# A decoder layer on eight cores: the residual and layer-norm stage of a query block is split into four pieces that are placed between the projections of the next block

## What is computed

```python
cq  = layernorm(x @ W_dq) ; q = [cq @ W_uq | rope(cq @ W_qr)]      # 16 heads of 128
ckv = layernorm(x @ W_dkv); k = [ckv @ W_uk | rope(x @ W_kr)]; v = ckv @ W_uv
attn = softmax(causal(q @ k.T / sqrt(128))) @ v
x1  = layernorm(x + attn @ W_o.T)
h   = silu(x1 @ (w_gate * s_gate)) * (x1 @ (w_up * s_up))
out = layernorm(x1 + (h @ w_down) * s_down)
```

## Time and profile before

| | us |
|---|---|
| profiled execution, whole | 8303.3 |
| its span on the slowest core (core 4) | 8301.6 |
| spans of the other seven cores | 8216.7 to 8294.2 |
| two timed runs | 8458.29 and 8760.03, median 8609.16 |
| PE busy in the span | 5968.6 (72%) |
| ACT busy | 2493.1 (30%) |
| DVE busy | 1747.0 (21%) |

### The profile page before, as it was taken

One profiled execution on the slowest core, in us unless ns is written; L12 is line 12 of the kernel. 1 busy time (PEld: TensorE's weight loads), 2 busy tenths in 40 slices (PEclk: granted clock), 3 DMA queues, 4 the chain that ended last, 5 costly groups with the idle time before them and its releaser, 6 DMA issues.

```text
span 8301.6 us, 76583 instructions; the slowest of 8 cores (8216.7 to 8301.6 us)
## 1 busy us (share of the span) xinstructions
PE 5968.6 (72%) x24816; PEld 2356.7 (28%) x24816; DVE 1747.0 (21%) x2859; ACT 2493.1 (30%) x4029; POOL 833.0 (10%) x1482
## 2 busy tenths in 40 slices
PE   1555558686485288438853888399999949999992
PEld 1222223233112112111221112144444424444441
DVE  0233322100131121111111110122322242222224
ACT  1222224311271175137612775111111111111111
POOL 1000000000000000000000000021212102121220
PEclk9877778888768678768886889699999979999996
DMA  4311131323213212321133222332323243232222
GB/s 103 75 59 62 39 78 63 79 69 93 46 36 87 72 45 61 76 79 54 47 84 82 61 58 68 102 91 61 83 71 82 72 137 82 72 82 72 75 78 76
DMA packets 411044, 603.61 MB, mean 73 GB/s; under 512 B 118952, under 2 KB 315002, under 8 KB 394020
## 3 DMA queue, kind: packets, MB, share of 16 engines
q0 software_dynamic: 213792, 344.37, 17.2%
q1 hardware_dynamic: 196868, 254.34, 9.4%
HBM read 461.87 MB, written 95.07 MB: 67 GB/s over the span
## 4 chain that ended last, share of the span: by engine, by line
PE 58%; DMA 17%; ACT 9%; DVE 8%; issue 5%; SPq 2%; POOL 1%; ACTq 0%; DVEq 0%; POOLq 0%
PE pq L272 57%; SPq L113 2%; DVE stats L289 2%; DMA wotr<-wots 2%; DMA wstr<-wqcat 1%; DMA vrows<-evst 1%; ACT U L1148 1%; DMA wstr<-wdq 1%; DMA wots<-wost 1%; DMA xf<-x1s 1%; DMA ckvts<-ckvTst 1%; DMA xa<-xkv 1%; PE pq L276 1%; DMA ckvT_sb<-ckvts 1%; DMA x1ts<-x1Tst 1%
## 5 line engine op out<-in xcount | busy, mean ns | idle before, releaser
L272 PE MATMUL pq<-x1T,gsl 128*128 128x512 bf16 x4096 | 930.0, 380 | 146.6 <-ACT gT L1452 107.5
L272 PE MATMUL pq<-x1T,usl 128*128 128x512 bf16 x4096 | 925.8, 379 | 0.0
L272 PE MATMUL pq<-dsl,fT 128*128 128x512 bf16 x4096 | 889.2, 379 | 50.2 <-DVE fT L1485 50.2
L1148 ACT ACTIVATE U<-pq,nch_sb 128x512 bf16<-128x512 f32 x1280 | 852.9, 685 | 219.1 <-PE pq L272 211.6
L1529 DVE TENSOR_TENSOR acc<-pq,acc 128x512 f32<-128x512 f32 x960 | 595.8, 682 | 303.7 <-PE pq L272 303.7
L272 PE MATMUL pq<-U 128*128 128x512 bf16 x1280 | 553.8, 433 | 145.0 <-ACT U L1148 109.7
L1452 ACT ACTIVATE gT<-pq,sgt_sb 128x512 bf16<-128x512 f32 x256 | 175.9, 687 | 1528.9 <-PE pq L272 1526.4
L272 PEld LDWEIGHTS pq<-x1T,gsl 128*128 128x128 bf16 x4096 | 401.5, 98 | 633.6 <-issue 153.5
L272 PE MATMUL pq<-QT,U 128*128 128x512 bf16 x1280 | 558.7, 438 | 17.2 <-DMA U<-kts 17.2
L272 PEld LDWEIGHTS pq<-dsl,fT 128*128 128x128 bf16 x4096 | 400.6, 98 | 538.7 <-issue 65.0
L272 PE MATMUL pq<-U,ones_cb 128*1 128x512 bf16 x1280 | 539.0, 421 | 0.0
(11 more groups left out here) (137 smaller groups left out, 4485.7 us busy)
## 6 DMA issues: line engine op xcount, KB each, us to landing
gsl<-wg POOLq DMA_DIRECT2D x512, 128.0 KB, 2.5
usl<-wu POOLq DMA_DIRECT2D x512, 128.0 KB, 2.5
dsl<-wd POOLq DMA_DIRECT2D x128, 512.0 KB, 4.8
xa<-xkv SPq DMA_DIRECT2D x32, 1024.0 KB
wotr<-wots SPq DMA_DIRECT2D x128, 256.0 KB, 2.6
ckvT_sb<-ckvts SPq DMA_DIRECT2D x160, 128.0 KB
vrows<-evst SPq DMA_DIRECT2D x128, 128.0 KB, 1.8
wstr<-wdq POOLq DMA_DIRECT2D x64, 256.0 KB, 3.6
```

What stands on the lines that cost most here:

```text
L272: h.matmul(o, a, b, start=s1, stop=s2)), waits, incs)
L1148: h.activation(out=o, in_=i, func=AF.Exp, bias=bb, scale=1.0)),
```

## The change

The function for the stage becomes one for a chunk, `x1_chunk(s_)`, and `pend_x1` a list of four such calls and one that collects the waits for `bendw`. In the next block the first chunk is taken from the list ahead of the first projection, the second ahead of the second projection, the third after the evictions of its first half, and what is left (the fourth chunk and the waits) where the whole stage stood. The code of a chunk is the same. After the last block the list is worked off at once, as before. Blocks 0 to 2 are thus split, block 3 is not.

```diff
-        pend_x1 = None
+        pend_x1 = []
...
             xtr = g_xTq.cw()
+            if pend_x1:
+                pend_x1.pop(0)()
             for dc in range(16):
...
                     if db == 1:
                         g_cqbf.freed(g_cqT)
+            if pend_x1:
+                pend_x1.pop(0)()
             cqtr = g_cqT.cw()
             for oh in range(2):
...
                         if oc == 15:
                             g_rope.freed(g_QT)
+                if oh == 0 and pend_x1:
+                    pend_x1.pop(0)()
             qtread = g_QT.cw()
 
-            if pend_x1 is not None:
-                pend_x1()
-                pend_x1 = None
+            while pend_x1:
+                pend_x1.pop(0)()
...
-            def x1_stage(n=n, aor=aor):
-                for s_ in range(4):
-                    i = s_ % 2
+            def x1_chunk(s_, n=n, aor=aor):
+                i = s_ % 2
...
+            def x1_fin():
                 bendw.clear()
...
-            pend_x1 = x1_stage
-        if pend_x1 is not None:
-            pend_x1()
+            pend_x1 = ([lambda s=s, f=x1_chunk: f(s) for s in range(4)] +
+                       [x1_fin])
+        while pend_x1:
+            pend_x1.pop(0)()
```

More of the change, by code:

```diff
@@ new lines, in x1_chunk @@
+            def x1_chunk(s_, n=n, aor=aor):
+                i = s_ % 2
+                c.dma("sync", xqr[i],
+                      self.xq[n * 512 + s_ * 128: n * 512 + (s_ + 1) * 128, :],
+                      list(g_xqr[i].pw()) + list(aor), g_xqr[i].pi(16))
+                c.emit("vector", (lambda h, o=x1pre[:, s_ * D:(s_ + 1) * D],
+                                  a=x1pre[:, s_ * D:(s_ + 1) * D], b=xqr[i]:
+                                  h.tensor_add(o, a, b)),
+                       list(g_xqr[i].cw()) + list(g_x1p.cw()), g_x1p.pi())
+                g_xqr[i].freed(g_x1p)
+                x1v = x1pre[:, s_ * D:(s_ + 1) * D]
+                c.emit("vector", None, g_x1f.pw(), ())
+                self.ln_chain(x1v, D, x1v,
+                              g_x1lv, g_x1ls, g_x1f, pre_gate=g_x1p,
+                              pre_ready=g_x1p.cw(), stats_base=10,
+                              junk=junkA2)
+                c.dma("sync",
+                      self.x1s[n * 512 + s_ * 128: n * 512 + (s_ + 1) * 128, :],
+                      x1v, g_x1f.cw(), g_x1d.pi(16))
+                for db in range(4):
+                    si = db % 2
+                    for k in range(4):
+                        hc = db * 4 + k
+                        w = []
+                        if k == 0:
+                            w = list(ptrb.pw()) + list(g_x1f.cw())
+                        self.tr(self.pb[7][:, k * 128:(k + 1) * 128],
+                                x1v[:, hc * 128:(hc + 1) * 128], self.iff[:],
+                                w, ptrb.pi() if k == 3 else ())
+                    c.emit("scalar", (lambda h, o=x1Tst[si][:],
+                                      i=self.pb[7][:, 0:512]:
+                                      h.copy(o, i)),
+                           list(ptrb.cw()) + list(g_x1T[si].pw()),
+                           g_x1T[si].pi())
+                    ptrb.freed(g_x1T[si])
+                    if db == 3:
+                        g_x1f.freed(g_x1T[si])
+                    col = n * 512 + s_ * 128
+                    for k in range(4):
+                        hc = db * 4 + k
+                        c.dma("sync", self.x1ts[hc * 128:(hc + 1) * 128,
+                                                col:col + 128],
+                              x1Tst[si][:, k * 128:(k + 1) * 128],
+                              g_x1T[si].cw() if k == 0 else (),
+                              g_x1d.pi(16), first=k == 0)
+                    g_x1T[si].freed(g_x1d)
```

## The result

| | before | changed |
|---|---|---|
| profiled execution, us | 8303.3 | 8184.9 |
| span of its slowest core | 8301.6 | 8183.2 |
| spans of its eight cores | 8216.7 to 8301.6 | 8138.0 to 8183.2 |
| all executions timed | 26: 8283.1 to 9009.5, median 8746.1 | 27: 8169.2 to 8901.7, median 8664.2 |

What follows compares the result with a forecast made beforehand. Bound: one chain per chunk through SP's in-order queue (sum, norm, store, small stores, next load). 270.6 saved, less 131.4 of stalls and 28.9 of slower stream, is 110.3 off 8303.3: 8193 us, own range 8164 to 8260, whole range 8130 to 8510.

Steps and rivals of the forecast that it cites:

- What bounds it, and what goes: Stage: chunks form one chain through SP's queue, 30 us each; first to fourth sum vanishes in three blocks, 270.6 us.
- The stalls: Projections: PE waits for each moved chunk's norm and transposes, 14.4, 15.3 and 14.4 us; 131.4 us in three blocks.
- table load: ACT's 1.28 us load ahead of the square root moves before the first projection; the norm behind it gets 1.3 back.
- cold start: Second half of the second projection starts slow after its stall, like the first half: 1 us more per block.
- The cost that the trace did not show: Moved transfers slow the projections' weight stream 3.2 us per chunk, nine chunks 28.9 us, bounds 0 and 95.6.
- The rule of the Trainium skill: SyncE and GpSimd transfers share 16 engines and interleave, so the moved load costs time; with separate engines, 8164 us.
- The sum: Whole kernel: 110.3 us off the profiled execution's 8303.3, giving 8193 us, 1.3% less.
- The time in microseconds: Whole kernel: 8193 us, whole range 8130 to 8510; a median lifted by 306 us would read 8499.
- More is hidden: Rival: norm's front overlaps PE's work, each moved chunk costs only 8.77 us of transposes; 8112 us; chance 0.13.
- The load is still late: Rival: moved chunks still wait for their loads, the old 30 us per chunk return; near 8303 us; chance 0.05.
- The weight stream collapses: Rival: transfers keep weight tiles' trips long, projections up to twice as long, 325 us in all; 8489 us; chance 0.05.
- What would show it: Signs in the changed profile: no sum waits for its load, about 60 us of 326 left, from the last block.

Runs made afterwards that it cites:

- experiment 5: Kernel before, stage whole in its old place, only the next chunk's load issued ahead of this chunk's stores on SP: 8159.9 us, ratio to before 0.984.
- experiment 1: Changed kernel with the 1 MB loads of chunks 1 to 3 left out in the three split blocks: 8159.2 us.

## Why the prediction was right, and where it was wrong

**What bounds it, and what goes.** Right. The 30 us per chunk were a chain through SP's queue with the load as its last link; experiment 5, which cuts only this link, took a third off it. What vanished is not measured by itself. With the other terms as measured below it comes to 112.3 + 3 x 41.8 + 35.5 = 273.2 us, against 270.6.

**The stalls.** Right, and a little high. Measured in the first split block: 13.9 less the 1.3 of the table load that the first norm no longer makes, 15.2 and 14.0, together 41.8 with no cold start; forecast 42.8 without it. The table load moved as forecast (ACT loads it at 2607.67, ahead of the first projection).

**The cost that the trace did not show.** Nearly right in size: 28.9 and 3 for the cold start were forecast, and the three projections' stretches grew by 8.9 + 26.6 = 35.5 us (the second without its gaps), 3.0 for a chunk in the first projection and 4.4 in the second. The mechanism names only a part of it. I had the stream stand still while the load fills the DMA engines, so that PE would wait. It did, and one tile's trip took 7.3 to 8.4 us in place of 3.6 to 4.1 where I had said 1 us more for two or three tiles. But over the nine stretches (medians of eight cores) the waits grew by only 15 us, from 111.7 to 126.4, and the matmuls' own time by 22, from 200.8 to 222.8. The granted clock fell with it: 0.94, 0.89 and 0.96 in the first projection and the two halves before, 0.90, 0.82 and 0.84 in the changed kernel, 0.95, 0.88 and 0.88 without the loads. That the longer waits bring the lower clock is likely, but no run holds the one and changes the other. The term thus came out close partly by luck: the waits alone were half of it. The rule of the Trainium skill that I weighed there ("DMA: Bandwidth & Descriptors", "Issuing engines are not separate DMA queues") agrees with the trace: a load started by SyncE doubled the trip of a tile started by GpSimd.

**The sum.** 110.3 us were forecast. The stretches gave 112.3, the profiled executions 118.4, the ratio 1.2% (0.8 to 1.7) against 1.3%.

**The time in microseconds, and the step that failed.** The median of all executions, 8664.2, lies outside my range of 8130 to 8510. The failed step is in "The sum": "the median 306. A median lifted in the same way would read 8499." I took the lift of a median over the profiled execution, 306 us, from two runs, and it is this term that was mis-sized. Over 26 runs the kernel before has a median of 8746.1, 443 above its profiled execution; the changed kernel's is 479 above its own. With that lift my own forecast reads 8193 + 443 = 8636, 28 us off. The range was built on the profiled execution, with its top end from two executions; it should have been given either for one of these figures or up to the 8760 that stood among the two. The change's own effect was forecast rightly; the level of the median was not.

**The rivals.** "More is hidden" did not happen: each chunk paid its norm as well. "The load is still late" did not: no projection waited for a sum's load. "The weight stream collapses" did not, since a load meets one or two tiles and not eight; experiment 1 puts it at 2.7 us per load. What was missing is the change's alternative, a reordered load, which gets the same gain by other means.

**What would show it.** I wrote that about 60 us of waits for `U<-xq` would be left. 135.4 were. The 72 over are idle time of DVE that the profile puts down to whatever came last; I took an attribution for a cost.

## What to carry to other kernels

When a stage shows all engines idle, follow the queue that issues its transfers before moving the stage: here a load stood behind 16 stores that it had nothing to do with, and issuing it first was worth at least about as much (1.6%) as splitting the stage over three places of the next block (1.2%), and left only some 25 us for the split to gain. Work that is moved between two pieces of an in-order engine's stream costs the whole of its latency there, 14 to 15 us for 4 us of transposes. Issuing the loads early did not shorten these stalls (14.8 us ahead of the first projection with and without it), since it is the norm that is waited for. And a weight stream with two buffers, each trip exposed, is both the place where moved transfers hurt and the larger prize: two more buffers took a third off the projections.

## What the runs showed that I had not expected

A 256 KB tile's trip went from 3.6 us to 7.3 and 8.4 when a 1 MB load was issued within 0.3 us of it, though the two together bring in only 1.25 MB. With four tiles in flight the median trip was 5.8 us and the stream was yet faster by a third. More of what the moved transfers cost went into slower matmuls, at a lower granted clock, than into waits (22 and 15 us). And of 27 executions of one and the same kernel the whole spread was 9%, seven times the effect of the change.
